# Block 0's first write prepared in attention's last slot, and one reciprocal moved behind its slot's exponentials

## Time and profile before

| | us |
|---|---|
| median of the runs | 2167.06 (2167.05, 2167.06, 2171.42) |
| the profiled execution's own time | 2159.65 |
| its span | 2157.7 |
| PE busy | 1922.2 (89%) |
| DVE busy | 1314.0 (61%) |
| ACT busy | 891.5 (41%) |
| POOL busy | 478.6 (22%) |

### The profile page before, as it was taken

How to read it: one execution, slowest core, us unless ns; L and a number is a source line. 1 busy time by engine, 2 the same in 40 slices (tenths; PEclk the granted TensorE clock), 3 DMA queues, 4 the chain that set the end, 5 groups by cost and what they waited for, 6 DMA issues and landing times.

```text
span 2157.7 us, 25293 instructions
## 1 busy us (share of the span) xinstructions
PE 1922.2 (89%) x9818; PEld 1349.9 (63%) x9818; DVE 1314.0 (61%) x1403; ACT 891.5 (41%) x1191; POOL 478.6 (22%) x362
## 2 busy tenths in 40 slices
PE   4789988999999973599899999999999999989997
PEld 0334446666666642377677777777776777666776
DVE  4476777555665539769468459567568566577100
ACT  4646654566776652261362530261530261432000
POOL 0013442768666800000000001100001100011010
PEclk9989998799999986799999999999999999999999
DMA  7547357999999732347468658668558667668676
GB/s 260 162 111 219 118 161 168 313 289 280 345 275 291 240 125 109 142 182 284 159 255 290 228 145 245 201 265 304 207 152 245 213 250 276 239 161 238 159 175 134
DMA packets 156283, 464.72 MB, mean 215 GB/s; under 512 B 34176, under 2 KB 34816, under 8 KB 138752
## 3 DMA queue, kind: packets, MB, share of 16 engines
q1 hardware_dynamic: 123568, 324.16, 47.7%
q0 software_dynamic: 30432, 128.46, 19.3%
q10 hardware_dynamic: 2160, 10.43, 1.4%
HBM read 323.79 MB, written 139.20 MB: 215 GB/s over the span
## 4 chain that ended last, share of the span: by engine, by line
PE 43%; DVE 7%; DMA 6%; ACT 4%; issue 2%; SPq 0%; POOL 0%; DVEq 0%; POOLq 0%; ACTq 0%
PE ps L1846 16%; PE ps L1656 8%; PE ps L1658 7%; PE ps L1657 7%; DMA sign_h<-sign_h_scratch 4%; DMA up<-up_s_scratch 2%; PE ps L1715 1%; PE ps L1724 1%; ACT L1875 1%; PE ps L1676 1%; DVE Y L2169 1%; PE ps L1765 1%; PE ps L1753 1%; ACT E_attn L1899 0%; DVE E_attn L2081 0%
## 5 line engine op out<-in xcount | busy, mean ns | idle before, releaser
L1846 PE MATMUL ps<-XH,sign_h 128*128 128x512 f32 x768 | 308.3, 401 | 16.9 <-DMA sign_h<-sign_h_scratch 12.2
L1846 PE MATMUL ps<-XL,sign_h 128*128 128x512 f32 x768 | 301.6, 393 | 0.0
L1222 DVE TENSOR_REDUCE maxes<-ps 128x1 f32<-128x512 f32 (+3 forms) x384 | 190.6, 552 | 134.3 <-PE ps L1062 97.1
L1166 ACT ACTIVATE probs<-ps 128x512 f32<-128x512 f32 (+3 forms) x384 | 178.3, 490 | 130.5 <-PE ps L1089 105.9
L1656 PE MATMUL ps<-ZH,up 128*128 128x512 f32 x512 | 205.2, 401 | 16.7 <-DVE ZL L2194 8.9
L1658 PE MATMUL ps<-ZH,up 128*128 128x512 f32 x512 | 200.9, 392 | 0.0
L1657 PE MATMUL ps<-ZL,up 128*128 128x512 f32 x512 | 200.8, 392 | 0.0
L1846 PEld LDWEIGHTS ps<-XH,sign_h 128*128 128x128 f32 x768 | 145.6, 190 | 65.5 <-DMA sign_h<-sign_h_scratch 16.8
L1846 PEld LDWEIGHTS ps<-XL,sign_h 128*128 128x128 f32 x768 | 145.6, 190 | 31.4 <-issue 1.9
L1569 POOL DMA_DIRECT2D out<-product_scaled x64 | 55.9, 874 | 443.0 <-DVE product_scaled L2263 443.0
L1104 PE MATMUL ps<-probs,values 128*32 128x512 f32 (+3 forms) x768 | 140.1, 508 | 0.0
(11 more groups left out here) (337 smaller groups left out, 4189.6 us busy)
## 6 DMA issues: line engine op xcount, KB each, us to landing
sign_h<-sign_h_scratch SPq DMA_DIRECT2D x256, 256.0 KB, 4.1
up<-up_s_scratch SPq DMA_DIRECT2D x58, 1024.0 KB, 6.4
proj<-proj_s_scratch SPq DMA_DIRECT2D x58, 640.0 KB, 3.9
X<-in_x_read POOLq DMA_DIRECT2D x16, 1024.0 KB, 9.0
xn_scratch<-X SPq DMA_DIRECT2D x16, 1024.0 KB, 12.7
sign_raw<-in_sign SPq DMA_DIRECT2D x32, 512.0 KB, 8.2
sign_h_scratch<-sign_high SPq DMA_DIRECT2D x32, 512.0 KB, 6.7
up_s_scratch<-weight_split SPq DMA_DIRECT2D x16, 1024.0 KB, 5.1
```

What stands on the lines that cost most here:

```text
L1166: eng.activation(PT[p % NPT][:, e, 0:w], ps[:, score_bank(v, p, e), 0:w], ACT.Exp, scale=HD ** -0.5).then_inc(ex.sem, ex.unit)
L1222: eng.tensor_reduce(MAXES[:, e, q, k0 // T:k0 // T + 1], ps[:, ring_bank(n, ("max", m)), 0:w], AX.X, ALU.max).then_inc(mx_read.sem, mx_rea ...
L1846: mm = eng.matmul(ps[:, sign_bank(m)], s[q][:, f], x[:, n], start=n + w == 0, stop=n == NF - 1 and w == len(operands) - 1, skip_group_chec ...
```

## The change

- Slots 1 to 16: `recip(n - 1, 0)` moves on ACT from behind the exponentials of step 9 to behind those of step 11 (and behind `row_out(n, 1)`); `head_out(n - 1, 0)` moves on DVE from step 10 to step 11.
- Slot 16: the small columns are summed first (`wall_sum(HC)` ahead of the last weighing of pair 14), and their split comes at step 0. The other four `wall_sum` and the first 8 of the 11 expansions are issued group by group in the order `USES`, all behind the scores of their group, in the three banks of the maxima. DVE makes the seven `factor(n)`; ACT makes the relus, the softplus of delta (`delta_exp` at step 8, `delta_ln` and `gates_exp_ln` after step 11), and after `recip(15, 1)` the reciprocals (`gates_recip`). DVE makes the two softplus sums before the last `head_out`.
- Block phase, block 0: `expansions`, `write` and `factors` skip what is already there. POOL loads channels 0 and 1 ahead of y and of the wall weights. The split of block 1's y moves behind channel 0 and its share of the read. ACT's copy `O0[1]` moves behind the last channel, ahead of the first weights' DMAs. Places in SBUF change, and block 1's `factors` waits for block 0's stored channels.

```diff
+        WALL_ORDER = (HC, *range(HC))
+        USES = [("wall", HC), ("wall", 0), ("exp", 0), ("exp", 1), ("wall", 1), ("exp", 2), ("exp", 3), ("exp", 4), ("wall", 2),
+                ("exp", 5), ("exp", 6), ("exp", 7), ("wall", 3)]
+        USE_AT = (USES[1:4], USES[4:7], USES[7:10], USES[10:])
...
+                def expansion(n):
+                    eng.wait_ge(wall_read_other.sem, wall_read_other.at(k=1))
+                    use_free(eng, ("exp", n))
+                    j = (0, 1, 2, 6)[n - HC] if n >= HC else -1
+                    eng.matmul(ps[:, use_bank(("exp", n))], EX[:, n if n < HC else 2 * HC + j], SM[j >= C - 1][:], start=True, stop=True,
+                               skip_group_check=True).then_inc(xp.sem, xp.unit)
...
+                    if n == PAIRS:
+                        wall_sum(HC)
                     if front(n - 2):
                         weigh_group(n - 2, LAST_GROUP)
...
-                            if n == PAIRS and p in WALL_AT:
-                                wall_sum(WALL_AT[p])
+                        for kind, i in USE_AT[g] if n == PAIRS else ():
+                            (wall_sum if kind == "wall" else expansion)(i)
...
-                        if n == PAIRS and p - 1 in WALL_AT and WALL_AT[p - 1] == HC:
+                        if n == PAIRS and p == 0:
                             small_highs()
+                        if n == PAIRS and p == 8:
+                            relu(HC)
+                            relu(HC + 1)
+                            delta_exp()
                         if front(n - 1) and p in JUDGE_AT:
                             judge(n - 1, JUDGE_AT.index(p))
                         if front(n - 2) and p == 4:
                             recip(n - 2, 1)
-                        if front(n - 1) and p == 9:
+                        if front(n - 1) and p == NSC - 1:
                             recip(n - 1, 0)
+                        if n == PAIRS and p == NSC - 1:
+                            relu(HC + 2)
+                            skip_out()
+                            delta_ln()
+                            gates_exp_ln()
                 recip(PAIRS - 1, 1)
+                gates_recip()
...
-                        if front(n - 1) and p == 10:
+                        if front(n - 1) and p == NSC - 1:
                             head_out(n - 1, 0)
-                        if n == PAIRS and p - 1 in WALL_AT:
-                            wall_out(WALL_AT[p - 1])
+                        if n == PAIRS and p == 0:
+                            wall_out(HC)
+                        if n == PAIRS and p % GROUP == GROUP - 1:
+                            for kind, i in USE_AT[p // GROUP]:
+                                if kind == "wall":
+                                    wall_out(i)
+                                elif i < HC + 3:
+                                    factor(i)
+                eng.wait_ge(ln.sem, ln.at(0, 1))
+                eng.tensor_tensor(W0["DL"][:], W0["DL"][:], W0["E0"][:], ALU.add).then_inc(sp_dl.sem, sp_dl.unit)
+                eng.wait_ge(ln.sem, ln.at(0, 2))
+                eng.tensor_tensor(W0["SP"][:], W0["SP"][:], W0["E1"][:, 0:3], ALU.add).then_inc(sp_dl.sem, sp_dl.unit)
                 head_out(PAIRS - 1, 1)
...
+                    load_h(0, 0)
+                    load_h(0, 1)
                     load_y(1)
-                    load_h(0, 0)
                     load_walls(0)
-                    for c in (1, 2):
-                        load_h(0, c)
+                    load_h(0, 2)
...
-                    for n in range(NE):
+                    for n in range(0 if s else HC + C, NE):
...
                     if v != 1:
                         eng.wait_ge(wr.sem, wr.at(s, 4))
+                    if v == 0:
+                        eng.activation(O0[1][:], ps[:, 0:HC], ACT.Copy).then_inc(o_0.sem, o_0.unit)
...
+                        if v == 0 and c == 0:
+                            eng.wait_ge(y_in.sem, y_in.at(0))
+                            eng.tensor_copy(YH[1][:], YIN[:]).then_inc(yh.sem, yh.unit)
+                            take_y(1)
```

More of the change, by code:

```diff
@@ L1890, in relu @@
                         eng.activation(SP[:, n - HC], ps[:, banks[n % len(banks)]], ACT.Relu).then_inc(relu_a.sem, relu_a.unit)
-                    relu(HC)
-                    yield
-                    relu(HC + 1)
-                    yield
-                    eng.wait_ge(xr.sem, xr.at(s, HC))
-                    table(LOG_EXP)
-                    for hc in range(HC):
-                        ins = eng.activation(E0[:, hc], E0[:, hc], ACT.Exp, bias=DUB[:, w, hc:hc + 1])
-                    ins.then_inc(chain.sem, 1)
@@ L1921, in write @@
-                    eng.wait_ge(chain.sem, chain.next())
-                    eng.activation(RG[:], RG[:], ACT.Exp, scale=-1.0).then_inc(rg_e_out.sem, rg_e_out.unit)
-                    yield
+                    if s:
+                        relu(HC)
+                        yield
+                        relu(HC + 1)
+                        yield
+                        eng.wait_ge(xr.sem, xr.at(s, HC))
+                        table(LOG_EXP)
+                        for hc in range(HC):
+                            ins = eng.activation(E0[:, hc], E0[:, hc], ACT.Exp, bias=DUB[:, w, hc:hc + 1])
+                        ins.then_inc(chain.sem, 1)
+                        yield
+                        relu(HC + 2)
+                        yield
+                        n = HC + C - 1
+                        eng.wait_ge(xp.sem, xp.at(s, n + 1))
+                        eng.activation(SK[:], ps[:, banks[n % len(banks)]], ACT.Copy).then_inc(sk.sem, sk.unit)
+                        yield
+                        eng.wait_ge(chain.sem, chain.next())
+                        table(LOG_EXP)
+                        eng.activation(E0[:], E0[:], ACT.Ln, bias=1.0).then_inc(ln.sem, ln.unit)
+                        yield
+                        eng.wait_ge(xr.sem, xr.at(s, HC + 3))
+                        table(LOG_EXP)
+                        eng.activation(E1[:, 0:3], E1[:, 0:3], ACT.Exp).then_inc(chain.sem, 1)
+                        eng.wait_ge(chain.sem, chain.next())
+                        eng.activation(E1[:, 0:3], E1[:, 0:3], ACT.Ln, bias=1.0).then_inc(ln.sem, ln.unit)
+                        yield
+                        eng.wait_ge(sp_dl.sem, sp_dl.at(s, 1))
+                        table(LOG_EXP)
+                        eng.activation(RG[:], SP[:], ACT.Ln, bias=t["eps"][:]).then_inc(chain.sem, 1)
+                        eng.wait_ge(chain.sem, chain.next())
+                        eng.activation(RG[:], RG[:], ACT.Exp, scale=-1.0).then_inc(rg_e_out.sem, rg_e_out.unit)
+                        yield
@@ L2070, in factors @@
                     E0, E1, DL, SP, RG = (tiles[n] for n in ("E0", "E1", "DL", "SP", "RG"))
-                    for n in range(HC + 3):
+                    if s == turn(1, 0):
+                        for b in (0, 2):
+                            eng.wait_ge(h_out[b].sem, h_out[b].at(0, H_COUNT[0][b]))
+                    for n in range(HC + 3 if s else 0):
                         bank = banks[n % len(banks)]
```

143 lines of the change are left out of this document (89 added, 54 removed).

## The result

The changed kernel took 2146.62 us (median of 6 runs, 2141.6 to 2156.0), the kernel before 2167.06 (median of 6, 2166.29 to 2171.42) on the same chip: a ratio of 0.9909, 95% interval 0.9886 to 0.9931. That is 20 us faster where 33 were forecast. The profiled execution of the changed kernel took 2141.6 us (span 2139.6, mean granted clock 0.950), the one of before 2159.65 (2157.7, 0.952): 18.1 us of span to account for.

The account below looks back on a forecast made before the run. It took PE's 15 waits for ACT's exponentials to bound the slots, and DVE's chain block 0's first write. 18.0 + 5.0 + 9.9 = 32.9 us off 2167.06 gave 2134; own range 2129 to 2139, wider range 2128 to 2147.

Parts of the forecast that it names:

- Part 1: Attention slots: moving half 0's reciprocal behind the exponentials removes 15 PE stalls of about 1.20 us, gaining 18.0 us.
- (a): Slots: the low clock stays because sparse row matmuls, not idle time, bring it; gain 27.9 us, 2139; chance 0.18.
- (e): Slots: the stall is only renamed, as row matmuls wait for the maximum; -9.9 us, 2157; chance 0.03.
- Part 2: Attention slots: three low clocks behind stalls vanish with the idle time, giving back 3 x 1.65 = 5.0 us.
- rival (d): Slot heads: shorter slots make operand loads late, PE stalls and falls to low clock; +12.9 us, 2180; chance 0.04.
- rival (c): Slots: DMA is their floor, so each gains 0.5 us instead of 1.2; total 17 us, 2150; chance 0.08.
- Part 3: Last attention slot: added expansions and two PE waits lengthen it, so the last `head_out` comes 6.0 us later.
- the pockets: Last slot: two PE idle waits for ACT's exponentials, behind `small_highs` and at step 8, about 1.5 and 2.1 us.
- 2 x 0.2 x 1.65 = 0.7: Last slot: expected low-clock cost behind two PE waits, from 3 in 15 stalls drawing one; 0.7 us.
- Part 4: Block 0's first write: channel 0 starts 14.1 us earlier, 6.5 behind the phase's start; y's split costs 3.5.
- The upper bound of +3 for parts 3 and 4: Last slot and first write: worst case +3 us, channel 0 waiting about 15 us from 800.8 for its data.

Follow-up runs that it names:

- The reciprocal alone: The kernel before with only half 0's reciprocal and its product on DVE moved behind the last exponentials; ratio 0.9937.
- the reciprocal with the later store: The kernel before with half 0's reciprocal and product moved and the store of split wall weights issued three slots later; ratio 0.9892.
- the kernel with the stalls put back: The changed kernel with half 0's reciprocal and its product put back to steps 9 and 10; ratio 0.9987.
- the store moved: The changed kernel with the 2.6 MB store of split wall weights issued three slots later, behind that slot's operand loads; 2131.89 us, ratio 0.9839.
- the kernel with y off DVE: The changed kernel with the wall store three slots later, `small_highs` two steps later, and block 1's y split on ACT and GpSimd; ratio 0.9846.
- the second profile: The changed kernel run and profiled once more, with no edit; ratio 0.9926 to the kernel before.

## Why the prediction was right in part and wrong in its size

- **Part 1** (-18.0) held: slots of 23.00 instead of 24.2 us, the reciprocal wholly beside the burst, no new wait of PE on ACT or DVE. The reciprocal alone and the reciprocal with the later store show it in a kernel without the rest of the change. Rivals (a) and (e), the stall or the clock that stays, fall with it.
- **Part 2** (-5.0) held: in no kernel in which the stalls are gone is there a low clock among the slots, but for the one behind the late load, and the kernel with the stalls put back has two again. The row matmuls stay in all of them, so the drops go with the idle time and not with them.
- **The step that failed** is rival (d), which I held unlikely with "No wait of PE on a DMA is among the waits of the stage". A list of waits shows what is late now, not what is nearly late. Its mechanism was right and its extent wrong: I priced a stall in each of 15 slots and left it out of the sum; it came in one slot, 4.1 us long with 7.6 lost to the low clock behind it: +11.7. The same hole is in the argument against rival (c), that a slot which moved 356 GB/s was no longer than one at 276. The loads issued in that slot had 3.9 us to spare (landed at 582.1, wanted at 586.04), but those of the slot ahead of it, at 333 GB/s, had 0.5: neither the rate nor the slot's length shows the margin, which could have been read from issue, landing and first use. The slots had no floor in DMA, though: all but two reached 23.0 with the change as it is, and all with the store moved (but for one of 23.7 in the kernel with y off DVE). The Trainium skill (DMA: Bandwidth & Descriptors, "Where 436 GB/s comes from") has about 358 GB/s as HBM's limit for a core. This trace does not bear that out: from the store's issue at 531.2 to 541.2 the changed kernel moved 409 GB/s, at a busy share of 1.01, and in the 13 us from there until the late load was there 297, at 1.02. So the measurement decides, and room can't be counted against 358.
- **Part 3** was short: the pockets came at 1.32 and 1.50 instead of 1.5 and 2.1, but I expected a low clock behind one of five such pauses, and in the profiled execution it came behind both: `head_out` +8.9 instead of +6.0. In the second profile it came behind the second alone, as in most others. So the term "2 x 0.2 x 1.65 = 0.7" was mis-sized: at 1.65 a time it was 3.3 here and 1.65 there, and up to `head_out` the two profiles do differ by 1.5 (57.08 and 55.56). The chance taken from stalls of 1.24 us did not hold for a pocket of 1.50, behind which it came each time.
- **Part 4** held nearly: channel 0 starts 7.3 instead of 6.5 us behind the phase's start, because the h that I wanted for its second operation is waited for ahead of its first. The order of issue did matter, in the direction of the change: with y first the wait is 3.37. The split of y costs 3.5 there, and GpSimd can't take it for less.
- **Together:** 18.0 + 5.0 + 6.8 - 11.7 - 0.4 = 17.7, against 18.1 measured between the two profiled executions. The upper bound of +3 for parts 3 and 4 doesn't follow from its own terms: 15 us from 800.8 is 815.8, 10.3 behind 805.5, which makes -0.3. That 2146.62 still lies within the range of 2128 to 2147 is luck: the range was made for a low clock that stays (a) and a bridge that gains nothing (b), and neither happened. With the store moved the lost 11 to 12 us come back, and the kernel is at 2131.89, ratio 0.9839: the version I would keep. Filling a pocket on top of it gives 2130.99 and 2130.60, which can't be told from it.
- **Open:** by medians and ratios the later store gives 15 to 19 us, and by start, slots and bridge of the two profiled executions 13.2, of which the slots are 11.7. Only one execution in each set of runs was profiled, so I can't say whether the slower runs of the changed kernel (up to 2156) had a second low clock or a later landing. Nor was it tried whether the raw table's 960 KB, moved away as well, would widen the 1.3 us that are left in the crowded slot; nor why the clock stayed low for 14 to 17 us behind the 4 us pauses and for only 3 to 4 behind a single pocket or stall.

## What to carry to other kernels

A stall taken out of each turn of a loop brings every load's deadline forward, but what a saturated engine or queue issues does not come forward with it. Before counting n times the stall, read the margin of each turn, above all of the one that carries extra transfers, and not of a typical one: last issue plus landing time against first use. If that margin is smaller than the deadline's shift, move the bytes that aren't urgent into an emptier turn first; behind the operands of the same turn is not enough.

## What the runs showed of the hardware that I had not expected

- Behind a pause of 4.1 us the granted clock was 0.50 for 17 us, of which PE was busy for 16.77. Behind stalls of 1.24 us a low clock came in 7 of 45 cases and behind a pocket of 1.50 us in 8 of 8; behind a stall it cost 1.65 us. So the price of a late load here was nearly three times its wait.
- A subtraction of 128x2048 on GpSimd (4.49 us) stretched DVE's subtraction of the same size beside it from 2.29 to 6.57 us.
- Landing times of the 128 KB operand loads were the same (9.6 and 9.7 us) in two kernels whose slots differ by 1.2 us, and 7.0 us where the store was moved away: in this crowded stretch a load's landing followed what was queued, and not when it was wanted.
